# Rotated queries and keys of a two-layer model: row moments on ScalarE, row factors and a quarter of the low parts on GpSimd, and a new order of the work

## The reference, cut to what matters

```
x = _layernorm(x + _L0_ffn_ref(...), axis=-1)          # each token: minus mean, over root of variance
q = (x @ Wq.T + bq)                                     # 512 features: 16 heads of 2 x 16
k = (x @ Wk.T + bk)
v = (x @ Wv.T + bv)
q1, q2 = (_apply_rope(q1, cos, sin), _apply_rope(q2, cos, sin))
k1, k2 = (_apply_rope(k1, cos, sin), _apply_rope(k2, cos, sin))
# _apply_rope: concatenate([x1 * cos - x2 * sin, x1 * sin + x2 * cos])
```

## Time and profile before

| | us |
|---|---|
| median of 3 runs | 2239.15 |
| the profiled execution's own time | 2237.7 |
| its span in the profile | 2235.9 |
| the part of it from the first to the last rotated unit (first L1776 to the end of the last L1759) | about 181 |
| granted TensorE clock, mean over the span | 0.969 |

### The profile page before, as it was taken

How to read it: one execution, slowest core, us unless ns; L and a number is a source line. 1 busy time by engine, 2 the same in 40 slices (tenths; PEclk the granted TensorE clock), 3 DMA queues, 4 the chain that set the end, 5 groups by cost and what they waited for, 6 DMA issues and landing times.

```text
span 2235.9 us, 49317 instructions
## 1 busy us (share of the span) xinstructions
PE 2091.0 (94%) x18242; PEld 1296.1 (58%) x18242; DVE 1758.2 (79%) x3087; ACT 1350.1 (60%) x2630; POOL 632.6 (28%) x761
## 2 busy tenths in 40 slices
PE   7999999899999999966776999999999999999998
PEld 5788887556666666645662333344334434448887
DVE  4777767856676676658988999889989999936878
ACT  6787776324545555533323899888888888862110
POOL 1000000003333433324661343533433243312000
PEclk9999999999999999988886999999999999998999
DMA  5444545663222222232432011011001101100000
GB/s 186 148 141 163 164 142 198 192 225 67 40 58 39 41 42 40 39 102 106 164 121 92 31 63 34 31 60 37 31 31 61 35 31 65 38 21 10 19 20 29
DMA packets 93352, 176.49 MB, mean 79 GB/s; under 512 B 16593, under 2 KB 64721, under 8 KB 91457
## 3 DMA queue, kind: packets, MB, share of 16 engines
q1 hardware_dynamic: 79488, 154.57, 20.1%
q0 software_dynamic: 13632, 18.77, 5.3%
HBM read 105.99 MB, written 66.78 MB: 77 GB/s over the span
## 4 chain that ended last, share of the span: by engine, by line
PE 58%; DVE 15%; issue 3%; ACT 2%; DMA 2%; SPq 1%; POOL 0%; DVEq 0%; ACTq 0%; POOLq 0%
PE PS L2414 12%; DVE NM L2295 7%; PE PS L58 6%; PE PS L60 6%; PE PS L59 6%; PE PS L2496 6%; PE PS L2439 5%; PE PS L1539 4%; PE PS L1582 2%; DVE TT L1776 2%; PE PS L1543 2%; PE PS L2434 2%; PE PS L2367 1%; DVE X L2686 1%; PE PS L2460 1%
## 5 line engine op out<-in xcount | busy, mean ns | idle before, releaser
L2295 DVE TENSOR_REDUCE NM<-PS 128x2 f32<-128x1024 f32 (+3 forms) x608 | 678.8, 1161 | 60.0 <-PE PS L2439 55.9
L2200 ACT ACTIVATE E<-PS 128x512 f32<-128x512 f32 (+2 forms) x1280 | 634.3, 554 | 115.0 <-PE PS L2496 105.8
L2414 PE MATMUL PS<-E,VP 128*32 128x256 f32 (+1 forms) x5120 | 364.7, 370 | 1.5 <-ACT OT L2232 1.1
L2132 POOL TENSOR_SCALAR_AFFINE_SELECT E<-E 128x512 f32<-128x512 f32 x256 | 162.1, 635 | 291.1 <-ACT E L2200 291.0
L1127 ACT ACTIVATE HB<-HB,SCH 128x512 f32<-128x512 f32 (+1 forms) x142 | 79.5, 607 | 201.6 <-DVE SCH L1356 201.6
L2414 PEld LDWEIGHTS PS<-E,VP 128*32 128x32 f32 x5120 | 110.1, 109 | 147.7 <-issue 110.3
L2496 PE MATMUL PS<-QK 50*128 50x512 f16 (+3 forms) x1152 | 185.0, 332 | 4.2 <-DVE X L2319 2.1
L2439 PE MATMUL PS<-QK 48*128 48x512 f16 (+3 forms) x1152 | 172.7, 338 | 7.4 <-DVE NM L2295 7.4
L58 PE MATMUL PS<-WALL,XIH 128*128 x426 | 161.6, 379 | 5.0 <-DVE HB L1342 2.3
L59 PE MATMUL PS<-WALL,XIH 128*128 x426 | 161.5, 379 | 0.0
L60 PE MATMUL PS<-WALL,XIL 128*128 x426 | 161.5, 379 | 0.0
(11 more groups left out here) (368 smaller groups left out, 4471.9 us busy)
## 6 DMA issues: line engine op xcount, KB each, us to landing
WIN<-in_we SPq DMA_DIRECT2D x24, 768.0 KB, 5.0
parts<-PP SPq DMA_DIRECT2D x32, 512.0 KB, 3.0
WALL<-pairs_of_weights SPq DMA_DIRECT2D x8, 1536.0 KB
QK<-parts SPq DMA_DIRECT2D x96, 128.0 KB
pairs_of_weights<-WPH SPq DMA_DIRECT2D x24, 384.0 KB, 2.3
pairs_of_weights<-WIN SPq DMA_DIRECT2D x24, 384.0 KB, 3.0
WALL<-pairs_of_weights SPq DMA_DIRECT2D x8, 768.0 KB
QK<-parts SPq DMA_DIRECT2D x96, 64.0 KB
```

The source lines that it names most:

```text
L2132: e.affine_select(out=E[:, m % NE, :, 0:128], in_=E[:, m % NE, :, 0:128], pattern=[[0, 4], [1, 128]], compare_op=ALU.is_ge, fill=0.0, base ...
L2200: e.activation(dst, src, ACT.Exp, scale=unit).then_inc(S.ex, 1)
L2295: e.tensor_reduce(dst, src, AX, ALU.max).then_inc(S.mx, 1)
L2414: a = e.matmul(PS[32 * jj:32 * jj + 32, 7, 512 - n + c0:512 - n + c1], VP[b % 2][:, kt, 17 * hd:17 * hd + 32], E[:, m % NE, jj, c0:c1], st ...
```

## The change

- `moments` for blocks 2 to 7 go from VectorE to ScalarE: a Copy of each tile with an accumulated sum, a Copy over four sums that gives minus the mean, a Square of each tile with minus the mean as bias and an accumulated sum. Their plain outputs go to a part of XH that is written again later. `root` of these blocks reads the sum of squares with a factor of 1/256. Blocks 0 and 1 stay as they were.
- NMR of blocks 2 to 7 is made on GpSimd, as minus the mean times the root.
- `low` runs two units behind on VectorE. Every fourth of the low parts (units 2, 6, ..., 30) is made on GpSimd, behind the two sums of the unit after it.
- `feed` and `BEFORE_K` are gone. A list `FIRST` says what comes ahead of unit 0 (more than before: block 1 as far as `norm`, and the sums of block 2). `ahead(i, place)` gives the jobs of turn i: turnings at every fourth turn (i%4 = 0 on ScalarE and VectorE, i%4 = 2 on TensorE), for one block a turn i%4 = 3 with the sums, i%4 = 0 with the squares and the root, i%4 = 1 with NMR and `norm`. ScalarE now does these jobs ahead of `high`, not behind it.
- Waits for low parts go through `low_made`, since two engines make them.

```
--- before.py
+++ after.py
@@ -1597,25 +1597,31 @@
 
 
 ROPE = group("""r_ld_mrc r_mrc r_ld_v r_x0 r_x1 r_x2 r_x3 r_x4 r_x5 r_x6 r_x7 r_vs0 r_vs1 r_pp0 r_pp1 r_pp2
-    r_vhi r_vlo r_mv r_rs r_nm r_xn pe_rx r_xhi r_xlo pe_ab tt r_sum r_hi r_lo pe_val r_val r_ones""")
-
-BEFORE_K = 9
+    r_vhi r_vlo r_mv r_rs r_nm r_xn pe_rx r_xhi r_xlo pe_ab tt r_sum r_hi r_lo r_lop pe_val r_val r_ones""")
+
 F16 = mybir.dt.float16
 
-
-def feed(n):
-
-
-    if n < 6:
-        g, i = 0, n
-    else:
-        g, i = (n - 6) // 7 + 1, (n - 6) % 7
-        if g == 8:
-            return "turn", 7, 0
-        if i == 2:
-            return "turn", g - 1, 0
-        i -= i > 2
-    return ("moments", g, i) if i < 4 else (("root", "norm")[i - 4], g, 0)
+FIRST = [("moments", 0, i) for i in QUAD] + [("root", 0, 0), ("norm", 0, 0)] + [("moments", 1, i) for i in QUAD] + [("turn", 0, 0), ("root", 1, 0), ("norm", 1, 0), ("moments", 2, 0), ("moments", 2, 1)]
+
+
+on_pool = lambda i: i % 4 == 2
+
+
+def low_made(S, i):
+
+    made = [on_pool(n) for n in range(i + 1)]
+    return (S.r_lop, made.count(True)) if on_pool(i) else (S.r_lo, made.count(False))
+
+
+def ahead(i, place):
+
+    g, k = (i + 1) // 4 + 2, (i + 1) % 4
+    todo = []
+    if g < 8:
+        todo += ([("moments", g, 0), ("moments", g, 1)], [("moments", g, 2), ("moments", g, 3), ("root", g, 0)], [("norm", g, 0)], [])[k]
+    if i % 4 == place and i < 28:
+        todo.append(("turn", i // 4 + 1, 0))
+    return todo
 
 
 def rope(nc, A, K, PS, D, own, before):
@@ -1641,7 +1647,6 @@
     x_ld, vs_st, pp_st = (S.r_x0, S.r_x1, S.r_x2, S.r_x3, S.r_x4, S.r_x5, S.r_x6, S.r_x7), (S.r_vs0, S.r_vs1), (S.r_pp0, S.r_pp1, S.r_pp2)
     nth = lambda t: 16 * (t // 2 + 1)
     place = lambda i: (i // 8, i // 2 % 2, i % 2, i // 4 % 2)
-    ahead = lambda i: [n for n in (BEFORE_K + 2 * i, BEFORE_K + 2 * i + 1) if n < 56]
     ctx.close()
 
     def sp(e, fetch_first):
@@ -1659,7 +1664,7 @@
 
         def store(i):
             b, qi, c, hf = place(i)
-            e.wait_ge(S.r_lo, i + 1)
+            e.wait_ge(*low_made(S, i))
             e.dma_start(D.PARTS[qi, b, c, :, :, 512 * hf:512 * hf + 512].rearrange("f p s -> p f s"),
                         PP[i % NP][:].rearrange("p a h s -> p (a h) s")).then_inc(pp_st[i % NP], 16)
 
@@ -1687,20 +1692,55 @@
             for h, op in ((0, ALU.subtract), (1, ALU.add)):
                 e.wait_ge(S.tt, 2 * i + h + 1)
                 e.tensor_tensor(z[:, h, :], z[:, h, :], z[:, 2 + h, :], op).then_inc(S.r_sum, 1)
+            for what, g, _ in ahead(i, 0):
+                if what == "norm":
+                    e.wait_ge(S.r_rs, g + 1)
+                    e.wait_ge(S.r_xn, g)
+                    e.tensor_tensor(NMR[:], K.ST[:, 0:4, 1], K.RS[:, 0:4], ALU.mult).then_inc(S.r_nm, 1)
+            if i >= 1 and on_pool(i - 1):
+                u = (i - 1) % NP
+                e.wait_ge(S.r_hi, i - 1 + 1)
+                e.tensor_tensor(PP[u][:, 1, :, :], TT[u][:, 0:2, :], PP[u][:, 0, :, :], ALU.subtract).then_inc(S.r_lop, 1)
 
     def act(e):
         leave(e, K, before)
 
-        def bring(n):
-            what, g, _ = feed(n)
+        def sums(g, pair):
+            e.wait_ge(x_ld[g], 16)
+            for j in pair:
+                c = 512 * g + 256 * (j % 2)
+                n = own.act.on(e.activation(XH[:, j // 2, c:c + 256], X[:, 4 * g + j, :], ACT.Copy, accum_out=K.ST[:, j, 0:1]))
+            return n
+
+        def squares(g, pair):
+            for j in pair:
+                c = 512 * g + 256 * (j % 2)
+                n = own.act.on(e.activation(XH[:, j // 2, c:c + 256], X[:, 4 * g + j, :], ACT.Square, bias=K.ST[:, j, 1:2], accum_out=K.ST[:, j, 2:3]))
+            return n
+
+        def bring(what, g, i):
+            if what == "moments" and g > 1:
+                if i < 2:
+                    n = sums(g, (2 * i, 2 * i + 1))
+                if i == 1:
+                    e.wait_ge(own.act.sem, n)
+                    n = own.act.on(e.activation(K.ST[:, 0:4, 1], K.ST[:, 0:4, 0], ACT.Copy, scale=-1.0 / 256))
+                    e.wait_ge(own.act.sem, n)
+                if i > 1:
+                    n = squares(g, (2 * i - 4, 2 * i - 3))
+                if i == 3:
+                    e.wait_ge(own.act.sem, n)
             if what == "norm":
                 e.wait_ge(S.r_nm, g + 1)
                 for j in QUAD:
                     a = e.activation(X[:, 4 * g + j, :], X[:, 4 * g + j, :], ACT.Identity, bias=NMR[:, j:j + 1], scale=K.RS[:, j:j + 1])
                 a.then_inc(S.r_xn, 1)
             if what == "root":
-                e.wait_ge(S.r_mv, g + 1)
-                rsqrt(e, own.act, K, K.RS[:, 0:4], K.MV[:, 0:4, 1], K.LV[:, 0:4], 1.0, 0).then_inc(S.r_rs, 1)
+                if g < 2:
+                    e.wait_ge(S.r_mv, g + 1)
+                    rsqrt(e, own.act, K, K.RS[:, 0:4], K.MV[:, 0:4, 1], K.LV[:, 0:4], 1.0, 0).then_inc(S.r_rs, 1)
+                else:
+                    rsqrt(e, own.act, K, K.RS[:, 0:4], K.ST[:, 0:4, 2], K.LV[:, 0:4], 1.0 / 256, 0).then_inc(S.r_rs, 1)
             if what == "turn":
                 c = slice(512 * g, 512 * g + 512)
                 for k in HALF:
@@ -1714,26 +1754,25 @@
             e.activation(PP[i % NP][:, 0, :, :], TT[i % NP][:, 0:2, :], ACT.Copy).then_inc(S.r_hi, 1)
 
         e.preload_act_table_set("natural_log_exp_and_others")
-        for n in range(BEFORE_K):
-            bring(n)
+        for what, g, i in FIRST:
+            bring(what, g, i)
         e.wait_ge(S.r_ld_mrc, 16)
         e.activation(K.MR[:], K.MRF[:], ACT.Copy).then_inc(S.r_mrc, 1)
         e.wait_ge(S.r_ld_v, 48)
         e.activation(WVH[:], WV1[:], ACT.Copy).then_inc(S.r_vhi, 1)
         for i in range(32):
+            for what, g, j in ahead(i, 0):
+                bring(what, g, j)
             if i > 0:
                 high(i - 1)
-            for n in ahead(i):
-                bring(n)
         high(31)
 
     def dve(e):
         leave(e, K, before)
 
-        def bring(n):
-            what, g, i = feed(n)
+        def bring(what, g, i):
             xs = [X[:, 4 * g + j, :] for j in range(4)]
-            if what == "moments":
+            if what == "moments" and g < 2:
                 e.wait_ge(x_ld[g], 16)
                 own.dve.on(e.bn_stats(K.ST[:, i, :], xs[i]))
                 if i == 3:
@@ -1743,7 +1782,7 @@
                     for j in QUAD:
                         a = e.bn_aggr(K.MV[:, j, :], K.ST[:, j, :])
                     a.then_inc(S.r_mv, 1)
-            if what == "norm":
+            if what == "norm" and g < 2:
                 e.wait_ge(S.r_rs, g + 1)
                 if g > 0:
                     e.wait_ge(S.r_xn, g)
@@ -1772,14 +1811,14 @@
                     e.wait_ge(S.pe_ab, 2 * i + o + 1)
                     if i >= NP:
                         e.wait_ge(S.r_sum, 2 * (i - NP) + h + 1)
-                        e.wait_ge(S.r_lo, i - NP + 1)
+                        e.wait_ge(*low_made(S, i - NP))
                     a = e.scalar_tensor_tensor(out=TT[i % NP][:, 2 * o + h, :], in0=PS[:, ka + o, :], scalar=BB[:, qi, 2 * c + o:2 * c + o + 1],
                                                in1=CS[qi][:, f, 512 * hf:512 * hf + 512], op0=ALU.add, op1=ALU.mult)
                 a.then_inc(S.tt, 1)
-            if i > 0:
-                low(i - 1)
-            for n in ahead(i):
-                bring(n)
+            if i > 1 and not on_pool(i - 2):
+                low(i - 2)
+            for what, g, j in ahead(i, 0):
+                bring(what, g, j)
             if i % 4 == 3:
                 j = i // 4
                 for h in HALF:
@@ -1798,21 +1837,20 @@
         leave(e, K, before)
         idn = K.IDN
 
-        def bring(n):
-            what, g, _ = feed(n)
+        def bring(what, g, i):
             if what == "turn":
                 for k in HALF:
                     e.wait_ge(S.r_xn, g + 1)
-                    if g in (1, 7):
-                        e.wait_ge(S.r_xlo, 2 * g - 1 + k)
+                    if g == 1:
+                        e.wait_ge(S.r_xlo, k + 1)
                     elif g > 1:
                         e.wait_ge(S.r_val, 2 * (g - 2) + k + 1)
-                    for i in QUAD:
-                        a = e.transpose(PS[:, 6 + k, 128 * i:128 * i + 128], X[:, 4 * g + i, 128 * k:128 * k + 128], idn[:])
+                    for j in QUAD:
+                        a = e.transpose(PS[:, 6 + k, 128 * j:128 * j + 128], X[:, 4 * g + j, 128 * k:128 * k + 128], idn[:])
                     a.then_inc(S.pe_rx, 1)
 
-        for n in range(BEFORE_K):
-            bring(n)
+        for what, g, i in FIRST:
+            bring(what, g, i)
         for i in range(32):
             b, qi, c, hf = place(i)
             ts = slice(1024 * b + 512 * hf, 1024 * b + 512 * hf + 512)
@@ -1825,16 +1863,14 @@
                 for k in HALF:
```

(11 more changed lines are left out.)

## The result

The changed kernel takes 2211.98 us (median of 4 runs, 2208.35 to 2216.34) against 2238.85 for the kernel before, timed beside it. The ratio is 0.9883, with a 95% interval of 0.9860 to 0.9906: 26 us less, between 21 and 31. The forecast was 2215.9, 23.3 less. The profiled execution took 2214.67 us (2214.4 were forecast) with a span of 2212.9; a second one, later, took 2210.78.

A forecast was written before the change was run, and what follows sets the result against it. VectorE was taken to set the pace. Units 0 to 23 28.9 us less, units 24 to 31 1.0 less, tail 1.6 more, stores 5 more: 23.3 less than 2239.15, 2215.9 us; range 2205 to 2230.

The forecast's parts named there:

- The pace: Units 0 to 23: VectorE sets the pace; a group of four units takes 16.8 us, 19.0 with the wait for norm.
- the 0.5 us for the port: Each group: 0.5 us for waits at the port that VectorE and GpSimd share, raising 16.3 to 16.8 us.
- Point 1: Low parts of every fourth unit on GpSimd: 2.4 us each, eight of them, behind the next unit's sums.
- Point 2: NMR on GpSimd: 0.25 us each, from 0.1 to 1.3 if it has to wait for a low part.
- point 4: ScalarE's list, norm ahead of high: VectorE waits 2.1 to 2.2 us before a low part, once in each of six groups.
- Point 3: Moments on ScalarE: eight accumulating passes at 0.7 us, 5.9 us per block with the small Copy, hidden behind the group.
- Point 5: Turnings at fixed places: cost nothing, hidden by 2.63 us of L1776; without that cover some 3 us each.
- Sum: Units 0 to 23 28.9 us less, units 24 to 31 1.0 less, tail 1.6 more, stores 5: 23.3 us less.
- Stores: Stores of PP landing late behind the fetches: 5 us taken off the gain, ends 0 and 13.
- The sign that I named: In the changed profile, waits of high for stores over 12 us in sum would show the prediction wrong (DMA).
- the port: Rival: VectorE's 18 low parts each wait for a whole GpSimd sum, up to 19 us more, 2235; half gives 2225; chance 0.10.
- a slow TensorE: Rivals, units 0 to 23: TensorE's clock low half the time, 2230, chance 0.07; low nearly throughout, about 2262, chance 0.03.

The follow-up runs named there:

- norm_behind_high: Changed kernel with ScalarE's norm behind high of the same turn: 2205.44 us.
- halves: Changed kernel with norm behind high, unit 30's low part on VectorE, each fetch in two halves three turns apart (turns 12 to 27): 2188.92 us.
- low_one_behind: Changed kernel with VectorE's low parts one unit behind in place of two, every fourth still on GpSimd: 2236.81 us.
- halves_low_vector: The kernel of halves with all low parts on VectorE, two units behind: 2199.36 us.
- nmr_on_vector: Changed kernel with only NMR of blocks 2 to 7 back on VectorE: 2212.77 us.
- moments_on_vector: Changed kernel with moments and NMR of blocks 2 to 7 back on VectorE: 2222.96 us.
- fetches_apart: Changed kernel with the attention stage's three fetches at turns 12, 17 and 22 in place of 12, 14 and 16: 2209.64 us.

## Why the prediction was right, point by point

- *The pace*: right. A group without stall was put at 16.8 us and is 16.8 (norm_behind_high, halves); with the wait for norm at 19.0, measured 18.4. But the 0.5 us for the port in it came out right by another cause. The port waits nearly vanished: the mean low part on VectorE is 1274 ns, against 1369 before. What took their place is the step of 1.34 us shown above. With low parts two units behind, L1815 of unit i waits for the low part of unit i-3, and that is now the instruction just ahead of it in two of a group's four units: 0.2 us, twice a group. Where L1815 waits for an earlier low part, the step is 1.13 (low_one_behind). I had not seen this wait; that it cost what I had set aside for the port is luck.
- *Point 1*: GpSimd's low part takes 2.14 us (2.4 taken). It was argued that the port would not bind; halves_low_vector shows it.
- *Point 2*: NMR 0.2 us on GpSimd, as taken. That it went made no difference to the median and 1 to 3 us to the stage (nmr_on_vector), which the sum has right only because it counts the wait of point 4 in full.
- *Point 3*: too dear, and hidden as said. A sum of 256 columns with its read of the accumulator takes 0.40 us of ScalarE's list, a square 0.49, not 0.7. I had the first unit 1.3 us late. It starts at 998.49 against 999.15, but this start moves from 996.3 to 1002.3 between the kernels, so one trace shows nothing. But the price of moments and NMR on VectorE, expected at 1.9 us a group in moments_on_vector, was too low by half: it was 3.6, and the chain aggregate, root, XH back to VectorE (1.1 us) was not in it.
- *Point 4*: right in place and cause, 1.54 us for 2.1 to 2.2, so 0.6 us too dear in each group. Norm behind high removes it.
- *Point 5*: put at nothing, and nearly right. VectorE waits 0.9 us for XH in three groups (at 1059.5, 1100.5 and 1122.9), 2.7 us in all. The 3.0 of group 0 were in the sum.
- *Sum*: units 0 to 23 were put at 116.4 + 5 for the stores, and took 120.8. Units 24 to 31 at 30.1, measured 31.6. The tail at 6.2, measured 5.4. The stage, 157.7 by these, took 157.75, and 155.8 in a second execution. That it fits to 0.1 us is luck: the three terms missed by -0.6, +1.5 and -0.8 us, and inside the first, point 4 and the start of group 0 were too dear by some 4 us, which the waits for XH and the stores, too cheap, gave back.
- *Stores*: 5 us taken. The two groups of the fetches lose 6.2 us against those of fetches_apart, but the whole stage gains only 1 to 3 us there. The sign that I named, waits of high over 12 us in sum, was wrong: they are 15.7, and 22.9 in a faster kernel. What counts is what is left of them on VectorE.
- *Rivals*: the port and a slow TensorE did not come. In units 0 to 23 TensorE is busy 83% of the time, against 72% before, and its granted clock is 0.94 against 0.85.

The sum gave 23.3 us. The profiled executions differ by 23.0, but the runs say 26, between 21 and 31, so the sum is right within the interval and more cannot be said. The two profiled executions of the changed kernel differ by 3.9 us of span: 2.0 in the stage, and about as much between the first reduction of the attention and the last stage, where nothing was changed.

## What to carry to other kernels

Work moved off the busiest engine is worth its time only if the order of the lists lets it be: with one unit's distance in place of two, the same relief was worth some 3 us instead of 26, and NMR's move was worth nothing in the median and 1 to 3 us of the stage. Before pricing a move, follow the chain that the moved value goes through and come back to the engine that sets the pace. And after a gain, look at what shares a queue with the stores: the same bytes in smaller portions, over more turns, took the last waits for stores off VectorE, 3 us of the stage. And a gain in the total is not yet a gain of the edit: in two of fourteen traces some 5 us came from the clock of a stage that no edit had touched.

## What was not expected of the hardware

- A store of 512 KB that is issued behind eight loads of a fetch landed 9.0, 10.3 and 13.2 us after its issue in the kernel before, instead of 3.0, though those loads are only 768 KB. Split in two and three turns apart, the same loads left no store later than 7.3 us; ScalarE still waited 12.2 us, VectorE not at all.
- A VectorE instruction that waits for the one just ahead of it on the same engine starts 0.2 us later (1.34 to 1.36 us behind a low part's start, against 1.13 to 1.15 where it waits for an earlier one).
- ScalarE's read of an accumulator has a record of 0.19 us, but the next pass starts 0.09 us after it: four sums with their reads start every 0.40 us.

```profile
1013.57 0.40 ACT L1712 ACTIVATE XH<-X 128x256 fp32r<-128x256 f32 x1
1013.88 0.19 ACT L1712 ACTIVATION_READ_ACCUMULATOR XH<-X 128x1 f32 x1
1013.97 0.40 ACT L1712 ACTIVATE XH<-X 128x256 fp32r<-128x256 f32 x1
```

- The mean granted TensorE clock over 25 us of the last stage was 0.73 to 0.86 in twelve traces and 1.00 in two, with the same program there; that is 5 us.
